# Tails of a four-layer convolution kernel: three images in flight instead of two, and a convolution cut into pieces

## The reference, cut to what matters

```python
x = x + _L0_conv_ref(_gn(x), ...)
x = x + _L1_conv_ref(_gn(x), ...)
x = x + _L2_conv_ref(_gn(x), L2_conv_gate_w, L2_conv_gate_b)
x = x + _L3_conv_ref(_gn(x), L3_conv_w1r, ..., L3_conv_conv_b)

# _L2_conv_ref
x_gray = jnp.mean(x, axis=1, keepdims=True)
dog = _conv(x_gray, gk1, pad) - _conv(x_gray, gk2, pad)
gx = _conv(dog, sobel_x, 1)
gy = _conv(dog, sobel_y, 1)
mag = jnp.sqrt(gx * gx + gy * gy + 1e-06)
att = jax.nn.sigmoid(mag * gate_w[0] + gate_b[0])
return x * (1.0 + ALPHA * att)

# _L3_conv_ref
g = _global_transform(c, w1, w2)
l = _local_transform(c, conv_w, conv_b)
return g * l
```

## Time and profile before

| | |
|---|---|
| median of 3 runs | 4096.14 us (4093.57 to 4103.01) |
| profiled execution | 4096.5 us, span 4094.7 us |
| TensorE busy | 3356.9 us (82%), granted clock 0.901 |
| VectorE busy | 2880.7 us (70%) |
| GpSimd busy | 2218.6 us (54%) |
| ScalarE busy | 1850.5 us (45%) |
| moved by DMA | 586 MB, mean 143 GB/s |

### The profile page before, as it was taken

The page is one execution under the profiler, slowest core; times in us unless marked ns, Lnnn a source line. Parts: engine busy times, 40 slices in busy tenths (PEclk is TensorE's granted clock), DMA queues, the critical chain, the costliest instruction groups (busy, mean ns, idle before and its releaser), DMA issues.

```text
span 4094.7 us, 90050 instructions
## 1 busy us (share of the span) xinstructions
PE 3356.9 (82%) x32900; PEld 1228.3 (30%) x32900; DVE 2880.7 (70%) x3545; ACT 1850.5 (45%) x2702; POOL 2218.6 (54%) x1099
## 2 busy tenths in 40 slices
PE   5669999389999999999999999999996467667444
PEld 2334444112122222222222222222221446555433
DVE  3643455389989899899899999899997464642034
ACT  0125655345555455555455555455552445553010
POOL 0000000079999999999999999999996000000000
PEclk9889999689999999999999999999998677778555
DMA  6574887566666656666566666566665234435487
GB/s 161 130 166 92 183 174 165 143 146 145 154 147 150 144 138 150 149 151 150 136 147 150 151 150 148 137 146 151 153 153 124 68 112 121 121 83 126 97 212 207
DMA packets 495588, 586.47 MB, mean 143 GB/s; under 512 B 72354, under 2 KB 335138, under 8 KB 489819
## 3 DMA queue, kind: packets, MB, share of 16 engines
q1 hardware_dynamic: 484596, 563.66, 59.6%
q10 hardware_dynamic: 10560, 16.93, 1.7%
HBM read 409.91 MB, written 184.54 MB: 145 GB/s over the span
## 4 chain that ended last, share of the span: by engine, by line
PE 30%; issue 28%; POOL 28%; DVE 5%; DMA 4%; ACT 4%; SPq 1%; ACTq 0%; POOLq 0%; DVEq 0%
POOL arena L1128 26%; PE ps L597 7%; PE ps L556 6%; PE ps L604 4%; PE ps L668 3%; ACT arena L887 2%; DMA arena<-l_dram 2%; PE ps L754 2%; POOL arena L1116 2%; PE ps L776 2%; DVE arena L1468 1%; PE ps L849 1%; PE ps L650 1%; DVE arena L1497 1%; PE ps L825 1%
## 5 line engine op out<-in xcount | busy, mean ns | idle before, releaser
L1422 DVE TENSOR_TENSOR arena<-ps,arena 128x1024 f32<-128x1024 f32 x1792 | 2107.4, 1220 | 204.0 <-PE ps L650 172.5
L1128 POOL TENSOR_TENSOR arena<-arena 128x1024 f32<-128x1024 f32 x896 | 1931.9, 2195 | 556.0 <-ACT arena L990 556.0
L668 PE MATMUL ps<-arena,w_mix 128*32 128x512 f32 x10752 | 1438.1, 607 | 79.4 <-POOL arena L1128 79.4
L990 ACT ACTIVATE arena<-ps 128x1024 f32<-128x1024 f32 x896 | 918.9, 1026 | 1025.4 <-PE ps L660 1014.6
L650 PE MATMUL ps<-arena,sel 48*128 48x512 bf16 x3584 | 702.0, 385 | 24.5 <-issue 15.2
L650 PEld LDWEIGHTS ps<-arena,sel 48*128 48x128 bf16 x3584 | 190.1, 93 | 944.9 <-issue 936.5
L660 PE MATMUL ps<-norms,opw 57*128 57x512 bf16 x1792 | 348.2, 384 | 49.1 <-ACT arena L922 17.5
L556 PE MATMUL ps<-arena,w_conv 32*32 32x512 f32 x9216 | 349.7, 657 | 43.4 <-issue 32.9
L668 PEld LDWEIGHTS ps<-arena,w_mix 128*32 128x32 f32 x10752 | 214.2, 108 | 467.5 <-issue 467.5
L1143 POOL COPY arena<-arena 32x130 f32<-32x130 f32 x32 | 9.3, 291 | 585.1 <-DVE arena L1470 584.1
L887 ACT ACTIVATE arena<-arena,nmr,rstd 128x128 f32<-128x128 f32 x768 | 301.1, 482 | 12.0 <-DVE nmr L1181 12.0
(11 more groups left out here) (151 smaller groups left out, 2168.1 us busy)
## 6 DMA issues: line engine op xcount, KB each, us to landing
arena<-pad SPq DMA_DIRECT2D x768, 260.0 KB, 7.7
split_dram<-arena SPq DMA_DIRECT2D x64, 768.0 KB, 3.6
arena<-split_dram SPq DMA_DIRECT2D x1536, 32.0 KB, 3.0
x_dram<-arena SPq DMA_DIRECT2D x16, 2048.0 KB, 7.0
l_dram<-arena SPq DMA_DIRECT2D x128, 256.0 KB, 4.6
arena<-x_dram SPq DMA_DIRECT2D x16, 2048.0 KB, 13.0
arena<-l_dram SPq DMA_DIRECT2D x32, 1024.0 KB, 17.1
pad<-arena SPq DMA_DIRECT2D x8, 2080.0 KB, 16.4
```

The source lines that it names most:

```text
L668: m = pe.matmul(ps[C * g:C * g + C, SUM + chunk % 2, :], w_mix[:, s, :], ring[:, (first + g // 2) % size, NPX * (g % 2):NPX * (g % 2) + NP ...
L990: nc.scalar.activation(ring_p[:, slot, :], ps[:, POOL_BANK:POOL_BANK + 2, :].rearrange("p a n -> p (a n)"), ACT.Tanh).then_inc(tanh_p, 1)
L1128: nc.gpsimd.tensor_tensor(slot, slot, pixels(chunk % 2, SPREAD[n // 2], n % 2), ALU.mult).then_inc(prod_p, 1)
L1422: nc.vector.tensor_tensor(slot, weights, pixels(par, ONCE[n // 2], n % 2), ALU.mult).then_inc(prod_d, 1)
```

## The change

- x1 has three buffers, layer 1's result in effect one (`ld[0]`; image 1 alone uses `ld[1]`). The attention's product is written over the normalised image, so it needs no `ld`. `xn3` has no border columns any more. To make room, two small buffers of the first layer share the memory of `dev` and `dev2`, and gn3 has its own slots of `rstd` and `nmr`.
- VectorE's turn i is: attention product, sum and statistics of image i (`attend`), sum, statistics and second norm of image i + 2, magnitude and gain of image i + 1, transposes of image i. The second norm is thus two images ahead.
- TensorE's and ScalarE's turn t is: gray sums, blur and Sobel of image t + 1, transforms of image t, convolution of image t - 1. The convolution halves are cut into pieces of 2, 2, 2 and 3 taps; those of the first half stand between the gray quarters, those of the second between the transform quarters.
- Image 0's loads are issued before the last chunk of layer 1 ends; those of images 1 and 2 where images 0 and 1 were loaded.
- The spectral weights wait for the transposes of image 6 and stand behind the stores of image 6's convolution.

```diff
-        xd = [planes(8192), planes(0)]
-        ld = [planes(12288), planes(4096)]
-        xn3 = [planes(16384, PW), planes(20544, PW)]
+        xd = [planes(8192), planes(0), planes(4096)]
+        ld = [planes(16384), planes(28996)]
+        xn3 = [planes(12288), planes(20480)]
...
@@ sync
-            def tail_in(t):
-                sp.dma_start(xd[t % 2], x1_dram[t]).then_inc(xd_loaded[t % 2], 16)
-                rows_in(ld[t % 2], image(l1_dram, t), ld_loaded[t % 2])
+            def x1_in(t):
+                sp.dma_start(xd[t % 3], x1_dram[t]).then_inc(xd_loaded[t % 3], 16)
+
+            def l1_in(t):
+                rows_in(ld[t == 1], image(l1_dram, t), ld_loaded[t % 2])
...
+                if n + 1 == B * CHUNKS:
+                    l1_in(0)
+                    x1_in(0)
...
-            tail_in(0)
-            tail_in(1)
+            l1_in(1)
+            x1_in(1)
+            x1_in(2)
...
+            sp.wait_ge(x2_done, 4)
+            l1_in(2)
             for t in range(B):
-                par = t % 2
-                if t >= 2:
-                    bands_out(t - 2, 0)
                 sp.wait_ge(x3_done, 4 * (t + 1))
-                sp.dma_start(x3_dram[t], xd[par]).then_inc(x3_stored[par], 16)
-                if t >= 2:
-                    bands_out(t - 2, 1)
-                if t + 2 < B:
+                sp.dma_start(x3_dram[t], xd[t % 3]).then_inc(x3_stored[t % 3], 16)
+                if t >= 1:
+                    bands_out(t - 1, 0)
+                if t + 3 < B:
+                    sp.wait_ge(x2_done, 4 * (t + 3))
+                    l1_in(t + 3)
+                if t >= 1:
+                    bands_out(t - 1, 1)
+                if t + 3 < B:
                     sp.wait_ge(gn3.out, 4 * (t + 1))
-                    sp.wait_ge(x3_stored[par], 16 * (t // 2 + 1))
-                    tail_in(t + 2)
-
-            sp.wait_ge(x3_stored[0], 16 * (B // 2))
-            sp.wait_ge(gn3.out, 4 * (B - 1))
+                    sp.wait_ge(x3_stored[t % 3], 16 * (t // 3 + 1))
+                    x1_in(t + 3)
+
+            sp.wait_ge(x3_stored[(B - 2) % 3], 16 * ((B - 2) // 3 + 1))
+            sp.wait_ge(bands_ready, B - 1)
+            sp.wait_ge(dfth_mm, 4 * (B - 1))
...
@@ tensor
-            for t in range(B + 2):
...
+            TAP_PARTS = ((0, 1), (2, 3), (4, 5), (6, 7, 8))
+            for t in range(-2, B + 1):
                 for n in range(4):
...
+                    if 0 <= t + 1 < B:
+                        gray_sum(t + 1, n)
+                    if t >= 1:
+                        conv3(t - 1, 0, TAP_PARTS[n])
+                if 0 <= t + 1 < B:
+                    blur(t + 1)
+                if 0 <= t < B:
                     after(pe, dftw_copy, 3 * t)
                     group_means(gn3, t)
+                if 0 <= t + 1 < B:
+                    sobel(t + 1)
+                if 0 <= t < B:
                     group_vars(gn3, t)
+                for n in range(4):
+                    if t >= 1:
+                        conv3(t - 1, 1, TAP_PARTS[n])
+                    if 0 <= t < B:
+                        dft_rows(t, n)
+                    if t + 2 < B:
+                        if n == 2:
+                            group_means(gn2, t + 2)
+                        if n == 3:
+                            group_vars(gn2, t + 2)
+                if 0 <= t < B:
+                    if t + 2 < B:
+                        pe.wait_ge(gn2.shifted, t + 3)
+                    dft_columns(t)
...
@@ scalar
+            for t in range(-2, B + 1):
+                if 0 <= t + 1 < B:
+                    after(act, bands_ready, t)
+                    after(act, dfth_mm, 4 * t)
+                    for q in range(4):
+                        normalise(gn2, t + 1, q, xn3[(t + 1) % 2], xd[(t + 1) % 3])
...
+                if t >= 1:
+                    conv3_out(t - 1, 0)
...
+                if 0 <= t < B:
+                    group_root(gn3, t)
...
+                for q in range(4):
+                    if 0 <= t < B:
+                        normalise(gn3, t, q, xn3[t % 2], xd[t % 3])
+                        if q:
+                            dft_out(t, q - 1)
...
+                if t + 2 < B:
+                    group_root(gn2, t + 2)
+                if 0 <= t < B:
+                    dft_out(t, 3)
+                if t >= 1:
+                    conv3_out(t - 1, 1)
+                if 0 <= t < B:
+                    spectrum(t)
...
@@ vector
+            for i in range(-2, B):
+                if i >= 0:
+                    attend(i)
+                    group_deviations(gn3, i, t)
+                if i == -1:
+                    magnitude(0)
+                    attention(0)
+                if i + 2 < B:
+                    tail_sum(i + 2)
+                if i >= 0:
+                    group_shift(gn3, i)
+                    group_scale(gn3, i, t)
+                if 0 < i + 1 < B:
+                    magnitude(i + 1)
+                if i + 2 < B:
+                    tail_stats(i + 2)
+                    group_deviations(gn2, i + 2, t)
+                    group_shift(gn2, i + 2)
+                if 0 < i + 1 < B:
+                    attention(i + 1)
+                if i + 2 < B:
+                    group_scale(gn2, i + 2, t)
+                if i >= 0:
+                    bands(i)
```

More of the change, by code:

```diff
@@ L502, in _ @@
                                  w[:, :, 4 * q:4 * q + 4, :].rearrange("i o x y -> i o (x y)")).then_inc(wm_loaded, 16)
-            for t in (B - 2, B - 1):
-                for half in range(HALVES):
-                    bands_out(t, half)
+            for half in range(HALVES):
+                bands_out(B - 1, half)
             sp.wait_ge(spec_copy, 8)
@@ L516, in _ @@
                 sp.wait_ge(l3_stored[par], 64 * B)
-                sp.wait_ge(x3_stored[par], 16 * (B // 2))
+            for t in range(B - 3, B):
+                sp.wait_ge(x3_stored[t % 3], 16 * (t // 3 + 1))
             with sp.Fori(0, B // 2) as i:
@@ L547, in group_vars, with conv @@
                 m.then_inc(gn.var, 1)
-            def conv(weights, tile, half, bank):
-                for tap in range(TAPS):
+            def conv(weights, tile, half, bank, taps=range(TAPS)):
+                for tap in taps:
                     dy, dx = divmod(tap, 3)
@@ L753, in dft_rows @@
                     at = 2 * KX * (c % QC)
-                    m = pe.matmul(ps[:, 6 + n % 2, at:at + 2 * KX], xn3[t % 2][:, c, 1:W + 1], const("dft_h"), start=True, stop=True)
+                    m = pe.matmul(ps[:, 6 + n % 2, at:at + 2 * KX], xn3[t % 2][:, c, :], const("dft_h"), start=True, stop=True)
                 m.then_inc(dfth_mm, 1)
@@ L1452, in attention, with magnitude @@
                 for q in range(4):
-                    nc.vector.tensor_tensor(quarter(ld[i % 2], q), tile[:, QC * q:QC * q + QC, 1:W + 1], gain, ALU.mult).then_inc(att_mul, 1)
+                    nc.vector.tensor_tensor(quarter(gated, q), quarter(gated, q), gain, ALU.mult).then_inc(att_mul, 1)
                 for q in range(4):
                     dve.wait_ge(att_mul, 4 * i + q + 1)
-                    nc.vector.tensor_tensor(quarter(xd[i % 2], q), quarter(xd[i % 2], q), quarter(ld[i % 2], q), ALU.add).then_inc(x3_done, 1)
+                    nc.vector.tensor_tensor(quarter(tile, q), quarter(tile, q), quarter(gated, q), ALU.add).then_inc(x3_done, 1)
                 for q in range(4):
                     dve.wait_ge(x3_done, 4 * i + q + 1)
-                    m = group_stats(xd[i % 2], QC * q, QC)
+                    m = group_stats(tile, QC * q, QC)
                 m.then_inc(gn3.stats, 1)
+            def magnitude(i):
+                dve.wait_ge(sob_sq, i + 1)
+                after(dve, att_mul, 4 * i)
+                nc.vector.scalar_tensor_tensor(out=ra[:, :], in0=r2[:, :], scalar=MAG_EPS, in1=rn[:, :], op0=ALU.add, op1=ALU.add).then_inc(mag_sum, 1)
+            def attention(i):
+                dve.wait_ge(att_tanh, i + 1)
+                nc.vector.tensor_scalar(ra[:, :], r2[:, :], 0.5, 1.5, ALU.mult, ALU.add).then_inc(gain_done, 1)
             def bands(i):
```

143 lines of the change are left out of this document (47 added, 96 removed).

## The result

| | before | changed |
|---|---|---|
| median | 4099.58 us (4 runs, 4093.57 to 4105.33) | 4051.72 us (4 runs, 4045.47 to 4056.3) |
| profiled execution: span | 4094.7 us | 4054.5 us |
| TensorE busy, granted clock | 3356.9 us, 0.901 | 3359.2 us, 0.909 |
| VectorE busy | 2880.7 us | 2880.1 us |
| GpSimd busy | 2218.6 us | 2273.6 us |

The ratio of the medians is 0.9882, with a 95% interval of 0.986 to 0.9904. The change gains some 48 us where I forecast 88: 4051.7 is above 4008 and above the range's end of 4042. The one odd number of the table is GpSimd's: 55 us more busy time for the same instructions.

A forecast was written before the change was run, and what follows sets the result against it. No engine was full: the tails were a chain of waits, 70.9 us per image. Spectral matmuls would start at 3239.5 + 321.5 + 53.8 + 75.6 = 3690.4 against 3778.59, 88.2 us earlier: 4008 us, range 3984 to 4042.

The forecast's parts named there:

- step 2: TensorE's first list in a round: gray quarters and first convolution half in pieces, 17.0 us plus 2.7 for clock, ending at 23.1.
- Steps 1 and 3 to 6: Rest of a tail round: first gray quarter, third norm, transform list, second norm and transposes, making 64.3 us against 70.9.
- step 5: TensorE's transform list after a 6.1 us pause: 15.7 us at full clock plus 3.4 lost at half rate, ending at 55.0.
- step 3: Blur and third norm's means after TensorE's first list, ready at 25.0; VectorE, done at 15.5, waits 9.5 us.
- rival C: Full rounds: operand shape changes cost and the clock rises late, 69.6 us a round, 4035 us; chance 0.13.
- rival D: Full rounds: x1 lands 6 us too late each time, 4038 us; chance 0.06.
- Rival B: Full rounds: TensorE's transform list runs wholly at half rate, +12.3 us a round, 4070 us; chance 0.06.
- Rival A: Full rounds: the clock survives TensorE's 6 us pause, 60.9 us a round, 3991 us; chance 0.13.
- Rival E: Full rounds: short pieces between waits keep both TensorE lists at half rate, 28.6 us more a round, 4186 us; chance 0.03.
- Rival F: Early load delays layer 1's last chunk and a misread wait eats the rest: under 8 us gained, 4092 us; chance 0.04.
- The start: From layer 1's end to the first transposes: first sum moves from 3162.7 to 3134.5, transposes end at 3239.5, -1.8 us.
- Rounds 6 and 7: Last rounds: 53.8 us for round 6, then 75.6 to the spectral matmuls, set by the spectral weights' landing.

The follow-up runs named there:

- experiment 2: Changed kernel with the eight halo copies issued by VectorE right behind its transposes instead of by GpSimd; 4013.9 us, ratio 0.9796 to the kernel before.
- experiments 1: Changed kernel with one added wait: VectorE's attention product starts only after GpSimd's halo copies; 4021.41 us, ratio 0.9814 to the kernel before.
- Experiment 3: Changed kernel with all four gray quarters first on TensorE, then the four pieces of the first convolution half; 4023.1 us, ratio 0.9819.
- experiment 6: experiment 2 with the third norm's means before the whole first convolution half, the second half in 2, 2, 5 taps between transform quarters; 3975.36 us, ratio 0.9698.
- experiment 5: experiment 2 with 24 unused 128x128 matmuls in TensorE's pause before the first transform quarter; 4006.65 us, ratio 0.9779.

## Why the prediction was off

The sum had four terms up to the spectral matmuls. Each beside the profile of the changed kernel, and of experiment 2, in which the halo is the only difference (us; T is the end of a round's transposes):

| | predicted | changed | experiment 2 |
|---|---|---|---|
| first transposes end | 3239.5 | 3244.85 | 3242.4 |
| rounds 1 to 5 | 321.5 | 348.4 | 324.6 |
| round 6 | 53.8 | 61.2 | 57.0 |
| from there to the spectral matmuls | 75.6 | 80.3 | 73.3 |
| spectral matmuls start | 3690.4 | 3734.8 | 3697.4 |
| gray quarter starts | T + 3.3 | T + 3.4 | T + 3.4 |
| list of step 2 ends | T + 23.1 | T + 29.7 | T + 24.1 |
| VectorE waits for the means | 9.5 | 16.2 | 8.5 |
| first transform quarter | T + 35.9 | T + 41.9 | T + 36.2 |
| shift of the second norm | T + 55.0 | T + 62.2 | T + 55.9 |

**The step that failed is step 2 of the round**: "TensorE's list is four gray quarters with the convolution half of image t-1 between them in four pieces", without a wait for the halo rows that the first piece reads. The change moves two things together that I took apart: it puts VectorE's two-input passes right behind the transposes, where GpSimd copies the halo, and it puts the first consumer of the halo 7 us behind the transposes (experiment 2, round 2). The kernel before shows each copy at 0.29 us, but beside 32-column operations; I took a duration from one neighbourhood into another. Round 2 of the changed kernel against the same round of experiment 2 gives the price: 4.5 us of wait, and 1.1 more since TensorE stays at half rate for longer (the first piece takes 4.08 instead of 3.22), 5.6 at the end of the list (29.7 against 24.1), which arrive at the end of the round as 6.3 (62.2 against 55.9). In rounds where the copies take 1.19 each the wait is 2.85 to 3.13 and the round 68.4 to 68.7. Rounds 1 to 5 came out 26.9 us longer than predicted, and 23.8 of these are the halo (348.4 - 324.6); experiments 1, 2 and 3 take it away in three ways. In round 6 it is 4.1 of 7.4.

**Steps 1 and 3 to 6 held.** Experiment 2 meets every one of them within 1 us: 64.9 a round against 64.3. The clock penalty of step 5, 3.4 in my sum, is 19.7 - 16.5 = 3.2 there, by the list without and with the filler, and the wait of step 3 is 8.5 instead of 9.5. The term that I set at nothing is not nothing: **changes of operand shape cost about 0.13 us each**. The convolution half starts 9.68 us before its successor where it runs whole (3435.38 to 3445.06, experiment 6), and in the changed kernel's pieces of 32 matmuls and 48 it takes 3 x 2.28 + 3.34 = 10.18, so (10.18 - 9.68) / 4 = 0.13 a piece. Experiment 3 has the same pieces one behind the other, and there the half takes 9.75 as in experiment 6: the cost comes with the other matmuls between the pieces, and what TensorE does in it no run shows. A gray quarter goes from 1.84 to 1.98 (3333.44 to 3335.42). That is 1.0 in step 2 and 0.8 in step 5 (16.5 for 15.7), the upper bound that the prediction named, "one matmul of 0.12 at each of 16 changes". A smaller slip is in step 5's "ends 2.7 and 5.4": 8.9 us at half rate cost 4.45, so rival C's 69.6 should have been about 68.6. x1 was never late: the loads landed 10.2 us after their issue by the median, faster than my 13 to 17, and no wait in the tails names one. That excludes rival D. Rival B (the list of step 5 at half rate throughout) is excluded by the third transform quarter of 2.00 us where the first took 3.68, rival C has half a truth, the changes of shape, but not the late clock. That the changed kernel's rounds of 69.7 on average meet its 69.6 is chance: in experiment 2, where the shapes change as often, they take 64.9. Rival A's 60.9 us a round is what the filler of experiment 5 reaches in three rounds. Rival E's mechanism, waits between short pieces that hold the clock down, is what happened to the first piece behind the wait for the halo: 1.1 us a round, where it needed 28.6. Rival F's "wait that I misread" is nearest in kind, but the wait for the halo ate 35 us of 88, not 80: against experiment 2 it is 23.8 in rounds 1 to 5, 4.1 in round 6 and 7.1 from there to the spectral matmuls, and the ratios say the same, (0.9882 - 0.9796) x 4098 = 35.

**The start** came out 5.35 late, 4.2 of it because layer 1 ended at 3138.72 instead of 3134.5. The first sum follows at 3138.64 with no wait for a load, as the sum had it. Over the profiles of this study the end of layer 1 lies between 3130.6 and 3143.1, for kernels that do not differ there, so I put this on the execution and not on the change.

**Rounds 6 and 7.** In round 6 I let ScalarE set the end, with "two copies of 0.57"; in experiment 2 ScalarE waits 0.69, 1.78 and 0.54 us for TensorE's transform quarters before its copies, 3.0 of the 3.2 us missing there: TensorE's half-rate list was the limit, as in a full round. In round 7 the convolution half begins T + 9.9 after a wait of 12.60 us for the halo, and ScalarE's copy of it and a table load stand before the third norm's root:

```profile
3675.93 2.12 ACT L1052 ACTIVATE arena<-ps,bias 128x1024 f32<-128x1024 f32 x2 [23.20 <-PE ps L568]
3678.06 1.28 ACT L902 ACT_TABLE_LOAD   x1
3679.36 0.23 ACT L902 ACTIVATE root<-sd 128x32 f32<-128x32 f32 x1
```

So normalising begins at T + 25.8 instead of 19.3. In the changed kernel the last wait before the spectral matmuls is then the copy of the last convolution half, "3734.78 ... [2.30 <-ACT arena L1052]" in TensorE's timeline, and not the weights. With the halo out of the way the weights decide as predicted, at T + 73.3 instead of 75.6. Behind the spectral matmuls the changed kernel took 319.7 us instead of 316.1; experiment 2 does not have these 3.6 (315.3). Some 2.2 of them lie between the spectral groups, where TensorE stops 1.7 to 3.1 us before each group without waiting for anything in the profile ("issue"): from the first to the last group it takes 59.5 us in the changed kernel, 57.3 before and 56.3 in experiment 2. Why these stops differ is open.

The terms add up: 5.35 + 26.9 + 7.4 + 4.7 + 3.6 = 48.0, which is the profiled execution's 4056.3 less 4008.3.

## What to carry to other kernels

When work moves on one engine, look at who runs beside it in its new place, and not only at who waits for it: a helper's duration in the trace holds only beside the neighbours it had there. Check every reader of a small helper result (halo rows, edge columns, copies) against the new order; a copy of 0.3 us that nobody waited for became 6 us of a 71 us round. And if a slow helper cannot be avoided, put its reader late: the same clash cost nothing once the gray quarters stood first.

## What the runs showed of the hardware

- GpSimd's copy of 32x130 values takes 0.29 us alone, beside small VectorE operations or beside VectorE's statistics, 1.17 to 1.19 us beside VectorE's two-input passes, one for each VectorE instruction of 1.22, or 9.12 us when it gets through only after all eight. Over four kernels 5 of 28 rounds began with the long form. In the long form VectorE's passes take 4.58 + 4.61 us; in the other they are slowed too, to 4.90 + 5.00. In both the copy begins 0.16 to 0.21 us behind the pass; what decides between the two forms I did not find.
- TensorE's 5.7 us pause costs 3.2 us in the list behind it, and filling it with 24 unused matmuls takes these away in three of five rounds, with the granted clock at 1.00.
- A change between 32-row and 128-row matmuls costs TensorE some 0.13 us, so spreading the convolution over eight pieces between other matmuls costs about 1.8 us of a round; in experiment 6 it is in four runs only.
